# The fifth tile's grouped convolution by three shared products, and the first five tiles in a new order, in an fp32 convolution-and-expert kernel

## The reference

```python
out = lax.conv_general_dilated(x, weight, ..., feature_group_count=GROUPS)
h = out + einsum('nd,od->no', c, c_weight)[:, :, None] + bias[None, :, None]
q = einsum('bsd,rd->bsr', h, Wq_w)              # 16 query values of a row
scores = einsum('bsr,er->bse', q, keys)         # 64 experts
gate = softmax over the 16 best scores, 0 elsewhere
z = einsum('bsd,nd->bsn', h, A_w)               # 512 = 64 experts x rank 8
x + einsum('bsn,on->bso', z * gate, B_w) * 2.0
```

## Time and profile before

| | us |
|---|---|
| median of 3 runs | 237.67 |
| lowest, highest run | 236.91, 238.66 |
| profiled execution, its time | 237.78 |
| profiled execution, its span | 235.8 |
| PE busy / weight loads busy | 231.0 / 206.4 |
| VectorE busy | 179.2 |
| ScalarE busy | 98.3 |

### The profile page before, as it was taken

The page is one execution under the profiler, slowest core; times in us unless marked ns, Lnnn a source line. Parts: engine busy times, 40 slices in busy tenths (PEclk is TensorE's granted clock), DMA queues, the critical chain, the costliest instruction groups (busy, mean ns, idle before and its releaser), DMA issues.

```text
span 235.8 us, 3992 instructions
## 1 busy us (share of the span) xinstructions
PE 231.0 (98%) x1398; PEld 206.4 (88%) x1398; DVE 179.2 (76%) x421; ACT 98.3 (42%) x245; POOL 1.6 (1%) x9
## 2 busy tenths in 40 slices
PE   8999999899999999999999999999999999999995
PEld 8988998598988989898898989889898988989884
DVE  1797799999969697996979698796969865644522
ACT  3897866255353253525424352532426241202100
POOL 2000000000000000000000000000000000000000
PEclk9999999999999999999999999999999999999999
DMA  6999017384644628263462816347282432616222
GB/s 196 379 403 379 10 47 224 100 276 161 177 152 100 244 70 258 77 186 147 105 235 71 276 58 194 138 105 234 72 240 93 121 146 51 220 45 222 92 89 89
DMA packets 22915, 38.22 MB, mean 162 GB/s; under 512 B 2544, under 2 KB 11120, under 8 KB 22896
## 3 DMA queue, kind: packets, MB, share of 16 engines
q1 hardware_dynamic: 22752, 37.89, 49.4%
q10 hardware_dynamic: 144, 0.08, 0.2%
HBM read 25.64 MB, written 12.32 MB: 161 GB/s over the span
## 4 chain that ended last, share of the span: by engine, by line
PE 93%; DVE 3%; issue 3%; ACT 0%; POOL 0%; DVEq 0%; POOLq 0%
PE p_z L608 36%; PE p_out L652 12%; PE p_out L653 12%; PE p_out L660 12%; PE p_conv L564 10%; PE p_conv L516 4%; PE p_out L608 3%; PE p_t L669 2%; PE p_out L516 1%; PE p_t L673 1%; DVE z_g L848 1%; PE p_t L622 1%; DVE h_lo L726 0%; DVE h_t L771 0%; DVE zt_lo L726 0%
## 5 line engine op out<-in xcount | busy, mean ns | idle before, releaser
L652 PE MATMUL p_out<-b_hi,zt_hi 128*128 128x512 f32 (+1 forms) x128 | 50.2, 393 | 0.0
L653 PE MATMUL p_out<-b_hi,zt_lo 128*128 128x512 f32 (+1 forms) x128 | 50.1, 393 | 0.0
L608 PE MATMUL p_z<-a_hi,h_hi 128*128 128x264 f32 x240 | 34.1, 285 | 1.0 <-DVE z_g L848 1.0
L608 PE MATMUL p_z<-a_lo,h_hi 128*128 128x264 f32 x240 | 35.0, 289 | 0.0
L660 PE MATMUL p_out<-b_lo,zt_hi 128*128 128x512 f32 (+1 forms) x128 | 34.5, 392 | 0.0
L608 PEld LDWEIGHTS p_z<-a_hi,h_hi 128*128 128x128 f32 x240 | 32.0, 188 | 2.6 <-issue 1.4
L608 PE MATMUL p_z<-a_hi,h_lo 128*128 128x264 f32 x240 | 34.2, 285 | 0.0
L608 PEld LDWEIGHTS p_z<-a_hi,h_lo 128*128 128x128 f32 x240 | 31.3, 188 | 0.0
L608 PEld LDWEIGHTS p_z<-a_lo,h_hi 128*128 128x128 f32 x240 | 31.0, 188 | 0.0
L343 ACT ACTIVATE h_hi<-h_t 128x1024 fp32r<-128x1024 f32 x16 | 17.0, 1064 | 31.5 <-DVE h_t L771 31.5
L726 DVE TENSOR_TENSOR x_lo<-x_blk,x_hi 128x1536 fp32r<-128x1536 f32 (+4 forms) x18 | 25.5, 1419 | 6.1 <-ACT x_hi L343 5.9
(11 more groups left out here) (100 smaller groups left out, 259.1 us busy)
## 6 DMA issues: line engine op xcount, KB each, us to landing
x_nat<-in_x_rows SPq DMA_DIRECT2D x16, 512.0 KB, 5.0
out_dram<-x_nat SPq DMA_DIRECT2D x31, 256.0 KB, 2.8
x_blk<-in_x_blocks SPq DMA_DIRECT2D x14, 516.0 KB, 4.4
z_dram<-a_raw SPq DMA_DIRECT2D x60, 64.0 KB, 1.8
a_raw<-z_dram SPq DMA_DIRECT2D x15, 256.0 KB, 3.8
a_raw<-in_a_wq SPq DMA_DIRECT2D x8, 264.0 KB, 6.3
x_nat<-in_b_w SPq DMA_DIRECT2D x4, 512.0 KB, 9.2
x_blk<-in_x_blocks SPq DMA_DIRECT2D x2, 258.0 KB, 3.9
```

The source lines that it names most:

```text
L608: mm = nc.tensor.matmul(z_bank(t, b)[:, 0:HB], h[:, t % 2, r, :], a[:, r, b * HB:(b + 1) * HB], start=k == 0 and r == 0, stop=k == 2 and r ...
L652: nc.tensor.matmul(dst, zt_hi[:, t % 2, c, :], b_hi[:, c, cols], start=c == 0, stop=False)
L653: nc.tensor.matmul(dst, zt_lo[:, t % 2, c, :], b_hi[:, c, cols], start=False, stop=False)
```

## The change

TW becomes 4, so that tile 4, too, is computed by shared products: TensorE has 9 matmuls for it instead of 12, VectorE's differ(4), add_shared(4) and a split_x(4) of 1536 elements are new, and ScalarE has add_u_shared(4) in place of add_u(4). The orders of VectorE and ScalarE from tile 1 to tile 3 are written anew. At the start the condition's term is computed in two pairs of groups (products_u, add_bias): the first pair's weights are copied by VectorE, the second's by GpSimd, and the second pair's matmuls stand inside the first convolution; seven matmuls of ones run instead of eight. SyncE issues z_in(1) ahead of load_rows(1) instead of behind it.

```diff
--- before.py
+++ after.py
@@ -15,7 +15,7 @@
 
 
 NT = 16
-TW = 5
+TW = 4
 TS = 3
 NN = 8
 NG = 4
@@ -233,6 +233,9 @@
         def z_bank(t, k):
             return (p_out if t == 1 else p_z)[:, k, :]
 
+        def u_bank(pair):
+            return p_z[:, 0, :] if pair else p_t[:]
+
 
         def scores_at(t):
             return z_bank(t, 0)[:, HB:HB + E]
@@ -299,8 +302,8 @@
             load_blocks(6)
             load_rows(0)
             z_out(1)
+            z_in(1)
             load_rows(1)
-            z_in(1)
             load_rows(2)
             load_rows(3)
             z_out(2)
@@ -333,9 +336,10 @@
             pool.wait_ge(s_iz, 1)
             nc.gpsimd.affine_select(out=ident[:], in_=ident[:], compare_op=ALU.not_equal, fill=1.0, base=0,
                                     pattern=[[-1, P]], channel_multiplier=1).then_inc(s_ident, 1)
-            pool.wait_ge(s_small, 16)
-            nc.gpsimd.tensor_copy(cw[:], sm[:, SMALL_CW:SMALL_CW + 64].rearrange("d (g c) -> d g c", c=CI).unsqueeze(2)
-                                  .to_broadcast([P, NG, R, CI])).then_inc(s_cw, 1)
+
+            pool.wait_ge(s_cw, 1)
+            nc.gpsimd.tensor_copy(cw[:, 2:NG], sm[:, SMALL_CW + 2 * CI:SMALL_CW + NG * CI].rearrange("d (g c) -> d g c", c=CI)
+                                  .unsqueeze(2).to_broadcast([P, NG - 2, R, CI])).then_inc(s_cw, 1)
 
         @block.scalar
         def _(act):
@@ -383,6 +387,8 @@
 
             def add_u_shared(t):
                 act.wait_ge(s_cs, t - TW + 1)
+                if t == 2 * TG:
+                    act.wait_ge(s_u, 2)
                 if t > TW:
                     act.wait_ge(s_hw, 2 * (t - TW))
                 for n in range(NN):
@@ -458,31 +464,31 @@
             split_x(3)
             add_u(2)
             take_q(0)
+            split_h(1)
             copy_q(0)
-            split_h(1)
             add_u(3)
-            split_x(4)
-            split_w(1)
             exp(0)
             split_h(2)
+            take_q(1)
+            split_w(1)
+            copy_q(1)
+            split_x(4)
+            sum_w(1)
             split_b(0)
             split_b(1)
-            take_q(1)
-            copy_q(1)
+            take_q(2)
+            exp(1)
+            copy_q(2)
+            split_h(3)
+            split_z(0)
             split_b(2)
-            exp(1)
-            take_q(2)
-            split_h(3)
-            copy_q(2)
             split_b(3)
-            split_z(0)
-            add_u(4)
-            sum_w(1)
+            add_u_shared(4)
             exp(2)
             split_x(5)
             take_q(3)
+            split_z(1)
             split_h(4)
-            split_z(1)
             for i in range(3, NT):
                 if i > 3:
                     take_q(i)
@@ -517,11 +523,20 @@
                                           start=first and s == 0, stop=last and s == 1)
                 return mm
 
+
+            def products_u(pair):
+                pe.wait_ge(s_cw, pair + 1)
+                for g in (2 * pair, 2 * pair + 1):
+                    mm = nc.tensor.matmul(u_bank(pair)[:, g % 2 * P:g % 2 * P + SMALL - SMALL_C], cw[:, g].rearrange("d r c -> d (r c)"),
+                                          sm[:, SMALL_C:SMALL], start=True, stop=True)
+                mm.then_inc(s_up, 1)
+
             def conv_first():
                 pe.wait_ge(s_whi, 1)
                 pe.wait_ge(s_xhi, 1)
                 for ab in range(2):
                     direct(0, 0, ab, 0, True, False)
+                products_u(1)
                 pe.wait_ge(*x_lo_done(0, 0))
                 for ab in range(2):
                     direct(0, 0, ab, 1, False, False)
@@ -590,6 +605,8 @@
                 if chunks[0] == 0:
                     if k == 0 and 1 in banks:
                         pe.wait_ge(s_hhi, t + 1)
+                        if t == 0:
+                            pe.wait_ge(s_u, 2)
                         if t == 1:
                             pe.wait_ge(*rows_done(1))
                         if t == 2:
@@ -665,15 +682,9 @@
                 out_low(t, k)
 
             pe.wait_ge(s_ones, 1)
-            for _ in range(8):
+            for _ in range(7):
                 nc.tensor.matmul(p_t[:, 0:P], ones[:], ones[:], start=True, stop=True)
-
-            pe.wait_ge(s_cw, 1)
-            for g in range(NG):
-                mm = nc.tensor.matmul(p_t[:, g * P:g * P + SMALL - SMALL_C],
-                                      cw[:, g].rearrange("d r c -> d (r c)"),
-                                      sm[:, SMALL_C:SMALL], start=True, stop=True)
-            mm.then_inc(s_up, 1)
+            products_u(0)
             conv_first()
             conv(1)
             conv(2)
@@ -866,15 +877,23 @@
                 nc.vector.scalar_tensor_tensor(out=x_nat[:, t % XN, lo:hi], in0=src, scalar=SCALING,
                                                in1=x_nat[:, t % XN, lo:hi], op0=ALU.mult, op1=ALU.add).then_inc(s_added, 1)
 
+            def add_bias(pair):
+                gs = slice(2 * pair, 2 * pair + 2)
+                dve.wait_ge(s_up, pair + 1)
+                nc.vector.tensor_tensor(u[:, gs], u_bank(pair)[:, 0:2 * P].rearrange("c (g n) -> c g n", n=P)[:, :, 0:32],
+                                        sm[:, SMALL_B + 2 * pair:SMALL_B + 2 * pair + 2].unsqueeze(2).to_broadcast([P, 2, 32]),
+                                        ALU.add).then_inc(s_u, 1)
+
+            dve.wait_ge(s_small, 16)
+            nc.vector.tensor_copy(cw[:, 0:2], sm[:, SMALL_CW:SMALL_CW + 2 * CI].rearrange("d (g c) -> d g c", c=CI)
+                                  .unsqueeze(2).to_broadcast([P, 2, R, CI])).then_inc(s_cw, 1)
             split_x(0, 0)
             split_w(0)
+            add_bias(0)
             split_x(0, 1)
-            dve.wait_ge(s_up, 1)
-            nc.vector.tensor_tensor(u[:], p_t[:].rearrange("c (g n) -> c g n", n=P)[:, :, 0:32],
-                                    sm[:, SMALL_B:SMALL_B + NG].unsqueeze(2).to_broadcast([P, NG, 32]),
-                                    ALU.add).then_inc(s_u, 1)
             split_x(1, 0)
             split_x(1, 1)
+            add_bias(1)
             split_keys()
             turn_h(0, 0)
             turn_h(0, 1)
@@ -886,12 +905,12 @@
             round_a(7)
             for r in range(2, R):
                 split_a(r)
-            split_x(3)
             turn_h(1, 0)
             turn_h(1, 1)
+            split_x(3)
             split_h(1)
+            turn_h(2, 0)
             copy_scores(0)
-            turn_h(2, 0)
             top_first(0)
             turn_h(2, 1)
             take_first(0)
@@ -900,46 +919,50 @@
             weigh(0)
             invert(0)
             gate(0)
+            turn_z(0)
             split_h(2)
-            turn_z(0)
+            differ(4, 0)
+            differ(4, 1)
+            turn_h(3, 0)
+            turn_h(3, 1)
+            sum_w(1)
+            split_w(1)
             split_x(4)
+            split_ws(1)
             copy_scores(1)
-            turn_h(3, 0)
             top_first(1)
-            turn_h(3, 1)
+            split_b(0)
             take_first(1)
-            split_b(0)
             top_second(1)
-            split_w(1)
+            split_b(1)
             take_second(1)
             weigh(1)
             invert(1)
             gate(1)
+            turn_z(1)
+            split_z(0)
             split_h(3)
-            split_z(0)
             copy_scores(2)
-            split_b(1)
             top_first(2)
             split_b(2)
             take_first(2)
-            turn_z(1)
             top_second(2)
             split_b(3)
-            sum_w(1)
             take_second(2)
             weigh(2)
-            split_ws(1)
             invert(2)
             gate(2)
             differ(5, 0)
             differ(5, 1)
+            add_shared(4, 0)
+            add_shared(4, 1)
             turn_z(2)
             turn_h(4, 0)
             turn_h(4, 1)
             split_x(5)
             split_q(3)
+            split_z(1)
             split_h(4)
-            split_z(1)
             add(0, 0)
             for i in range(3, NT):
                 if i + 2 >= NT:
```

## The result

The changed kernel took 239.32 us in the median of 9 runs (238.94 to 239.59), the kernel before beside it 237.46 (236.91 to 238.73). The ratio is 1.0073, with a 95% interval of 1.0051 to 1.0095: 1.2 to 2.3 us slower. The forecast was 239.7, or 2.0 slower. The profiled execution of the changed kernel took 239.0 us.

What follows compares the result with a forecast made beforehand. VectorE's list up to turn_q(3) was taken as the bound: 237.67 us plus 2.0 us of delay gives 239.7 us, with the start's 0.2 already in the anchor and the 0.70 hidden. Its own range was 239.2 to 240.4 us.

Steps and rivals of the forecast that it cites:

- What bounds the kernel: TensorE is busiest, but VectorE's list up to turn_q(3) is as tight and becomes the bound; chance 0.66.
- margin 0.20: At turn_q(3): VectorE's split_q(3) could be 0.20 us later before TensorE has to wait for it.
- Tile 4's convolution: 12 matmuls become 9: 0.70 us less for TensorE, hidden; VectorE pays 2.94 us more.
- The order from its last anchor: VectorE's new list from 33.16 us to split_q(3): z(3) 1.0 us later, turn_q(3) 2.0 us later.
- the anchor: x_hi of tile 4 from ScalarE's split_x(4), behind copy_q(1), ready at 33.13 us, fixes VectorE's list from there.
- the overlap of 0.09 us: On VectorE the next instruction starts 0.09 us before the previous ends, so starts, not full lengths, are the price.
- The start: Before the first convolution: one matmul of ones less and a shorter weight copy bring TensorE 0.2 us earlier (0 to 0.3).
- one fixed moment: At the start TensorE's clock rises from 1.2 GHz at the same moment, about 7.2 us; 0.3 us earlier becomes 0.17.
- TensorE as the bound: First rival: the new order wins back VectorE's added work, so 0.2 and 0.70 us both count: 236.8 us; chance 0.10.
- the second rival: gate(2) comes as before; only add_shared(4), 1.20 us less the margin of 0.20, remains: 238.7 us; chance 0.10.
- A fall of the clock in the new pauses: Third rival: TensorE's waits at split_z(0) and split_q(3) drop its clock, costing 1.7 us more: 241.4 us; chance 0.14.

Runs made afterwards that it cites:

- e5: The kernel before plus two 512-element subtractions on VectorE, result unread, between differ(5) and turn_z(2); 238.38 us, ratio 1.0020.
- e3: The changed kernel with half of add_shared(4) and turn_h(4) behind split_q(3) on VectorE, split_h(4) behind copy_q(3) on ScalarE; 238.84 us, ratio 1.0025.
- e10: The changed kernel with only differ(4), differ(5) and sum_w(1) moved to GpSimd; 238.68 us, ratio 1.0015.
- e11: The kernel before with ScalarE's exp(0) and split_h(2) ahead of split_x(4), exp(2) ahead of sum_w(1); 237.08 us, ratio 0.9971.
- e1: The changed kernel with tile 4 computed directly again (12 matmuls, no differ(4), no add_shared(4)); 238.10 us, ratio 1.0004.
- e4: The kernel before, old start, with tile 4 by shared products put into the old order; 239.03 us, ratio 1.0047.
- e14: e10 with ScalarE's split_x(4), split_w(1) and sum_w(1) straight behind split_h(2), ahead of take_q(1) and copy_q(1); 237.71 us, ratio 0.9996.
- e2: The kernel before with only the new start (condition's term in two pairs, seven matmuls of ones); 237.56 us, ratio 0.9989.
- e7: e4 with one half of add_shared(4) and turn_h(4) moved behind split_q(3), as in e3; 238.65 us, ratio 1.0017.
- e8: e7 with differ(4), differ(5) and sum_w(1) on GpSimd and ScalarE's list ordered for it; 238.49 us, ratio 1.0018.

## Why the prediction was right

**What bounds the kernel.** VectorE's list, not its share of busy time, set z(3) and turn_q(3), and the prediction had this mechanism right. e5 showed it for turn_q(3) without the change (0.95 us for 1.20 us of work, margin 0.20 read from the rows), e3 and e10 by taking work away again (0.95 us each), and e11 for z(3) from the other side.

**Tile 4's convolution.** The 0.70 us of TensorE are real (nine matmuls start between 36.98 and 38.92, each 0.24 us behind the last) and hidden, for TensorE then waits 1.5 us. e1 and e4 together tell where the loss lies: with tile 4 direct it is gone within 0.5 us, with tile 4 shared in the old order it is 1.1 us.

**The order from its last anchor.** copy_scores(1) was expected 3.84 us behind turn_q(1) (35.00 against 31.16), measured 3.87; z(3) 16.45, measured 16.49; turn_q(3) 22.4, measured 22.37. e10 and e14 showed that the anchor, x_hi of tile 4 behind copy_q(1), is a hold. The forecast split the loss into 1.0 ahead of z(3) and 1.0 behind it; e3 removed the second without the first. The single terms fit as well, so the sum isn't right by terms that cancel: from copy_scores(1) to turn_z(1), the gate of tile 1 with its two split_b, 5.09 us were forecast and 5.09 measured (34.35 to 39.44), and from copy_scores(2) to differ(5) 4.99 and 4.96. The distances between starts were the right price. The prediction said that the overlap of 0.09 us contradicts the Trainium skill, VectorE: DVE Perf Modes, The DRAIN you can't avoid; that went too far, for the same section adds that an instruction that isn't held starts earlier.

**The start** is the term that no run bears out. Its 0.2 us are below what can be told: e2 gives -0.3 us with 0.6 either way. In the changed kernel's profile turn_q(1) came 0.88 us sooner, and that is no work of the change: in e3, with the same start, it came at 31.49, behind the 31.36 of the kernel before. The first four loads of the first convolution there, from its timeline:

```profile
4.86 0.53 PEld L522 LDWEIGHTS p_conv<-x_hi,w_hi 128*128 128x128 f32 x4
```

They run at the pace of 2.4 GHz at 4.9 us. In e2, with the same start, they do not; the same line there:

```profile
5.00 0.93 PEld L521 LDWEIGHTS p_conv<-x_hi,w_hi 128*128 128x128 f32 x4
```

That is the pace of 1.2 GHz, as at 6.33 in the earlier trace rows. The profile's granted clock doesn't show this: it reads 1.00 from 4 to 7 us in the kernel before, the changed one and e2, so the level is read here from the lengths of the loads alone, 0.93 against 0.53 us. The time at which the pace rises differs between executions of the same start, and the prediction's assumption of one fixed moment doesn't hold.

**The size of the whole.** Distances say 2.2 us, the ratio 1.7 (1.2 to 2.3). Whether the rest of 0.5 is more than noise is not settled. Most kernels of the table lie lower in time than by distance, so the profiled execution of the kernel before seems to have a rather short stretch for its kind. A candidate is the way of z of tile 0 through DRAM, shown at e2: 3.11 us in the profile of the kernel before and 5.21 in that of e2, where turn_z(0) stands at the same place. In the changed kernel it took 3.12 us, and turn_z(0) stands 2.3 us earlier by its distance from turn_q(1), so that a long way would have time to spare; its runs lie within 0.65 us, those of the kernel before within 1.8. If the kernel before has the long way in some of its runs, they raise its median and make the loss look smaller. No kernel tested that by itself.

**The rivals.** TensorE as the bound (0.10) didn't come: in e7, with the wait at turn_q(3) undone, the matmuls still gained nothing. Nor did the second rival, gate(2) as before: z(3) was 1.24 us later behind turn_q(1). A fall of the clock in the new pauses didn't come either: behind the pause of 1.51 us the second matmul starts 0.31 us behind the first and the others 0.23 to 0.24 apart, the 0.234 of the kernel before, behind turn_q(4) the tiles follow at 13.74 us, against 13.75 before, and the mean granted clock was 0.999. By the Trainium skill, Perfetto Trace Analysis, Identifying the Most-Contended Engine, work on the engine with the highest occupancy comes first, and TensorE's is to be judged by the busy share of its weight loads. That share was 88%, still above VectorE's 76%, so the rule names TensorE either way; taken over the whole span it didn't foretell this time, since in the stretch from turn_q(1) to turn_q(3) VectorE's list was full.

## What to carry to other kernels

Before a change that moves work from the busiest engine to another, read the other engine's list between two fixed points, and look for the margin at its end, even where no wait is shown: with 0.20 us of margin, 1.20 us of work became 0.95 us of delay. Work taken away ahead of a fixed point gave nothing here (1.4 us in e10), and behind it nearly all (0.95 of 1.20 us). A wait inside the second engine's list can be worth more than work taken off the first: another order of ScalarE's exp gained 0.2 to 1.2 us in e11, where the three matmuls of a tile gained nothing. And where a way through DRAM differs by 2 us between executions, one profile's distances need a second kernel with the same order beside them.

## What the runs showed of the hardware

Single VectorE instructions took up to 0.93 us longer while GpSimd worked on SBUF (in e8 2.15 against 1.22 us and 1.11 against 0.22; in e10 1.72 against 1.22; in e14 1.10 against 0.22), one or two of many in each kernel. GpSimd's sum of 128 elements took 4.33 us in e8 and 3.5 to 3.6 in e10 and e14, though a difference of 512 took 1.3 to 1.5; the lengths on GpSimd are rough. And 256 KB on their way through DRAM, from the first of four writes to the read that follows their landing, took 3.1 to 3.2 us in eight profiles and 4.1 to 5.2 in six.
